# Attention, two feed-forwards and a decaying memory on one core: weights enter the scans as ratios, the next input is made ready early, and ScalarE squares what it rectifies

## The reference

```python
x = x + _layernorm(_L0_attn_ref(_layernorm(x), ...))   # attention
x = x + _layernorm(_L0_ffn_ref(_layernorm(x), ...))    # first feed-forward
x = x + _layernorm(_L1_attn_ref(_layernorm(x), ...))   # the memory
x = x + _layernorm(_L1_ffn_ref(_layernorm(x), ...))    # second feed-forward
```

```python
p_w = jnp.exp(log_p + log_tw)              # a weight per time and slot, 32 slots
phi = k_val[..., None] * theta             # 32 slots x 8 channels x 8 angles
den = jnp.cumsum(p_w[..., 0], axis=1)
num_re = jnp.cumsum(pwb * jnp.cos(phi), axis=1)
num_im = jnp.cumsum(pwb * jnp.sin(phi), axis=1)
inv = lax.rsqrt(jnp.maximum(den, 0.0001)); inv = inv * inv
out = jnp.sum(s_re * qr + s_im * qi, axis=-1)   # s = num * inv; likewise out_im
y = silu(y_re + y_im) @ W_out
```

## Time and profile before

| | us |
|---|---|
| median of 3 runs | 1694.96 |
| lowest, highest | 1694.31, 1700.07 |
| the profiled execution's own time | 1691.56 |
| its span, first to last instruction | 1689.7 |

### The profile page before, as it was taken

The page is one execution under the profiler, slowest core; times in us unless marked ns, Lnnn a source line. Parts: engine busy times, 40 slices in busy tenths (PEclk is TensorE's granted clock), DMA queues, the critical chain, the costliest instruction groups (busy, mean ns, idle before and its releaser), DMA issues.

```text
span 1689.7 us, 22269 instructions
## 1 busy us (share of the span) xinstructions
PE 1298.3 (77%) x7692; PEld 792.9 (47%) x7692; DVE 1330.3 (79%) x2794; ACT 960.4 (57%) x1637; POOL 564.5 (33%) x335
## 2 busy tenths in 40 slices
PE   4376886678779987988789988897799877865336
PEld 2244364435445554646455654564456455422214
DVE  4953347988788889987998899987989899778850
ACT  2165357744685578565865687457855794343301
POOL 1000301472054602570246314540546035505600
PEclk9589898779979998989899999999899989877668
DMA  5310223103311322131313131222203320012000
GB/s 181 75 38 1 63 45 100 59 24 83 87 60 38 75 65 88 38 87 38 95 57 77 31 100 59 68 52 63 96 25 75 71 82 26 13 61 78 13 0 13
DMA packets 62431, 101.38 MB, mean 60 GB/s; under 512 B 8192, under 2 KB 32144, under 8 KB 62320
## 3 DMA queue, kind: packets, MB, share of 16 engines
q1 hardware_dynamic: 62320, 99.95, 21.4%
HBM read 74.24 MB, written 25.69 MB: 59 GB/s over the span
## 4 chain that ended last, share of the span: by engine, by line
PE 33%; DVE 22%; ACT 12%; issue 12%; POOL 10%; DMA 8%; SPq 2%; POOLq 0%; DVEq 0%; ACTq 0%
PE ps L752 13%; PE ps L762 10%; POOL work L719 5%; DVE work L1304 4%; DVE work L1223 4%; DVE work L1313 3%; ACT work L1001 3%; DMA work<-weights 2%; ACT work L1008 2%; DVE norms L1134 2%; PE ps L833 2%; DMA work<-values 2%; POOL norms L687 2%; PE ps L815 2%; PE ps L890 2%
## 5 line engine op out<-in xcount | busy, mean ns | idle before, releaser
L719 POOL TENSOR_TENSOR work<-work 128x1024 f32<-128x1024 f32 x128 | 336.5, 2654 | 480.9 <-ACT work L1056 400.3
L1001 ACT ACTIVATE work<-work 128x384 f32<-128x384 f32 (+3 forms) x512 | 264.7, 558 | 168.7 <-DVE work L1223 167.8
L1304 DVE TENSOR_TENSOR_SCAN work<-ps,work 128x512 f32<-128x512 f32 x256 | 302.2, 1209 | 17.5 <-POOL work L719 17.0
L1223 DVE CUSTOM_DVE_ANT_0 work<-ps,work 128x384 f32<-128x384 f32 (+3 forms) x512 | 226.8, 485 | 109.1 <-PE ps L807 106.5
L815 PE MATMUL ps<-ident,work 128*128 128x128 f32 x1280 | 217.3, 298 | 53.8 <-DVE work L1223 44.5
L687 POOL TENSOR_TENSOR norms<-norms,power 128x4 f32<-128x4 f32 x64 | 71.3, 1114 | 498.8 <-DVE norms L1140 498.7
L815 PEld LDWEIGHTS ps<-ident,work 128*128 128x128 f32 x1280 | 160.1, 152 | 130.1 <-DVE work L1223 77.2
L1313 DVE TENSOR_TENSOR work<-work 128x1024 f32<-128x1024 f32 x128 | 215.2, 1681 | 5.1
L1008 ACT COPY work<-ps 128x512 f32<-128x512 f32 x320 | 181.2, 571 | 46.3 <-PE ps L815 46.2
L807 PE MATMUL ps<-work 96*128 96x384 bf16 (+3 forms) x512 | 132.5, 327 | 47.8 <-ACT work L1008 39.3
L752 PE MATMUL ps<-xTd,wf 128*128 128x512 f32 x256 | 126.0, 629 | 11.5 <-ACT xTd L966 7.9
(11 more groups left out here) (161 smaller groups left out, 1937.5 us busy)
## 6 DMA issues: line engine op xcount, KB each, us to landing
work<-values SPq DMA_DIRECT2D x64, 256.0 KB
work<-weights SPq DMA_DIRECT2D x64, 256.0 KB
scratch<-work SPq DMA_DIRECT2D x32, 384.0 KB, 5.1
work<-scratch SPq DMA_DIRECT2D x64, 192.0 KB, 3.7
work<-scratch SPq DMA_DIRECT2D x64, 128.0 KB, 4.0
x_in<-x SPq DMA_DIRECT2D x8, 512.0 KB, 3.4
work<-scratch SPq DMA_DIRECT2D x64, 64.0 KB, 4.0
weights<-work SPq DMA_DIRECT2D x8, 512.0 KB, 4.6
```

The source lines that it names most:

```text
L719: g_.tensor_tensor(wave, wave, pwr[:, slot, None, :].to_broadcast([P, MH, T]), ALU.mult).then_inc(*weighed[half].one)
L1001: i = s_.activation(part_of, part_of, ACT.Exp, scale=-1.0, bias=nmax[:, row:row + 1])
L1223: i = v_.tensor_tensor_reduce(sc[:, n % 4, at:at + nk], out_of(name)[:, at:at + nk], base_of(qt), -SCORE_SCALE, BIG, ALU.add, ALU.min, nma ...
L1304: v_.tensor_tensor_scan(ring[:, at, m, :], still.to_broadcast([P, T]), ring[:, at, m, :], 0.0, ALU.add, ALU.add).then_inc(*scanned.one)
```

## The change

It has these parts:

- **Ratios in the scans.** The weighted sum n(t) = n(t-1) + w(t) c(t) is replaced by s(t) = s(t-1) * w(t-1)/w(t) + c(t), so s = n / w. The scan reads the ratio from `pwr` (SBUF) and multiplies; `weigh` goes. The factor at the gate is now w / sum of w. The weights are bounded from below by 1e-20 so that they can divide.
- **Where ratios come from.** `total`: VectorE bounds the weights, scans and bounds their sum. SP stores both and loads them back spread over 128 partitions x 128 times, the weights twice, the second time one element earlier (`spread`). `ratio`: two reciprocals and two products of 128x128. SP stores the ratios in four pieces and the rates (`rates`), then loads the four `pwr` slots. A slot is free after the scans of its sine half.
- **Next input early.** `x_in` has two buffers; x[b+1] is loaded during attention b (`fetch`), its statistics and centring come near the end of the score tiles (`stats+`, `centre+`), its scaling and transposes around the output product (`norm+`, `xT+`). The output's statistics have a chain of their own in `norms`.
- **First feed-forward.** ScalarE squares right after rectifying, GpSimd no longer. The head of b + 2 (`fstats`, `fnorm`, `fxT`) stands before the last product of b, and `fnorm` waits for the transposes of b - 2 only.
- **q and k pieces** go to DRAM separately, q before k is computed.
- **Start.** Only `wo` is centred ahead (`means` 0, `N_WO` = 3 steps); the first output product waits for that alone. The rest of the preparation is interleaved with the first attention. In b = 0 every second transposed score tile is copied out by VectorE (20 copies).
- PSUM banks 5 and 6 are dealt out in program order over both dense halves, and `MERGE` is written anew for all engines.

```diff
@@ items
-    items = ["stats", "norm", "xT", "ckv", ("q", 0), ("q", 1), "qr", ("k", 0), ("k", 1), "kr", "pieces", ...
+    items = ["ckv", ("q", 0), ("q", 1), ("pieces", 0), "qr", ("k", 0), ("k", 1), ("pieces", 1), "kr", ...
+        if n == ALL - 4:
+            items += ["stats+", "centre+"] * after
+    items += ["attnT"] + ["norm+"] * after + ["out"] + ["xT+"] * after + ["ystats", "sum"]
...
-def on_act(m):
-    return True
+def on_act(b, m):
+    return b > 0 or m % 2 == 0
@@ MERGE, one line of each engine's
-        "a5 p10 a3 p12 a90 d a15 d a4 d a4 d a18 d a5 d a4 d a4 d a4 m2 a4 m2 a3 m a4 m2 a4 m2 a2 m2 a2 m a2 "
...
@@ SP
-                if item == "weights":
-                    need(sp, pw_ready, b, 1)
-                    sp.dma_start(weights[b], zs[:, None].to_broadcast([K, H, T])).then_inc(*p_saved.one)
+                if item == "total":
+                    need(sp, w_ready, b, 1)
...
+                    sp.dma_start(plain[1 + b * K * T:1 + (b + 1) * K * T].rearrange("(k t) -> k t", k=K), zs).then_inc(*w_saved.one)
+                    need(sp, tot_ready, b, 1)
+                    sp.dma_start(totals[b], total).then_inc(*tot_saved.one)
+                if item == "spread":
+                    need(sp, kv_saved[0], b, 1)
+                    need(sp, w_saved, b, 2)
+                    for before in (1, 0):
+                        at = 1 - before + b * K * T
+                        sp.dma_start(spread[:, 1 - before, :], plain[at:at + K * T].rearrange("(p t) -> p t", p=P)
+                                     ).then_inc(*spread_loaded.one)
+                    need(sp, tot_saved, b, 1)
+                    sp.dma_start(spread[:, 2, :], totals[b].rearrange("k (i t) -> (k i) t", i=TT)).then_inc(*spread_loaded.one)
+                if item == "rates":
+                    need(sp, ratio_ready, b, 1)
+                    for i in range(TT):
+                        sp.dma_start(ratios[b, :, :, i * P:(i + 1) * P],
+                                     spread[i:P:TT, 0, None, :].to_broadcast([K, H, P])).then_inc(*ratio_saved.one)
+                    need(sp, rate_ready, b, 1)
+                    sp.dma_start(rates[b].rearrange("k (i t) -> (k i) t", i=TT), spread[:, 2, :]).then_inc(*rate_saved.one)
@@ POOL
-                if item == "fc":
-                    is_drained(pool, b, f"fc{n}")
-                    g_.tensor_tensor(hid[:, n, :], hid[:, n, :], hid[:, n, :], ALU.mult).then_inc(*hid_sq.one)
-                if item == "weigh":
...
-                    g_.tensor_tensor(wave, wave, pwr[:, slot, None, :].to_broadcast([P, MH, T]), ALU.mult
-                                     ).then_inc(*weighed[half].one)
@@ PE, first output product
-                        pe.wait_ge(prep_step, N_PREP)
+                        pe.wait_ge(prep_step, N_WO)
@@ ACT
                 if item == "fnorm":
-                    need(act, g_sum, b - 2, 1)
+                    if b:
+                        is_filled(act, *((b - 2, "gxT1") if b > 1 else (0, "zxT1")))
...
+                    is_drained(act, b, f"fc{n}")
+                    s_.activation(hid[:, n, :], hid[:, n, :], ACT.Square, bias=zero[:, 0:1]).then_inc(*hid_sq.one)
@@ DVE
-                if item == "inv" and n == 0:
-                    need(dve, pw_ready, b, 1)
+                if item == "total":
+                    need(dve, exp_ready, b, 1)
+                    v_.tensor_scalar(zs, zs, LEAST, None, ALU.max).then_inc(*w_ready.one)
...
-                    step(inv_step, v_.tensor_scalar(total, total, 1e-4, None, ALU.max))
-                    v_.reciprocal(total, total).then_inc(*inv_ready.one)
+                    v_.tensor_scalar(total, total, 1e-4, None, ALU.max).then_inc(*tot_ready.one)
+                if item == "ratio":
+                    need(dve, spread_loaded, b, 3)
+                    before, now, den, per = (spread[:, i, :] for i in range(4))
+                    v_.reciprocal(den, den)
+                    step(ratio_step, v_.reciprocal(per, now))
+                    v_.tensor_tensor(before, before, per, ALU.mult).then_inc(*ratio_ready.one)
+                    v_.tensor_tensor(den, den, now, ALU.mult).then_inc(*rate_ready.one)
...
-                    need(dve, weighed[half], b, r + 1)
-                    v_.tensor_tensor_scan(ring[:, at, m, :], still.to_broadcast([P, T]), ring[:, at, m, :], 0.0,
-                                          ALU.add, ALU.add).then_inc(*scanned.one)
+                    need(dve, (cos_waved, sin_waved)[half], b, r + 1)
+                    need(dve, pw_loaded[slot], b, use)
+                    v_.tensor_tensor_scan(ring[:, at, m, :], pwr[:, slot, :], ring[:, at, m, :], 0.0,
+                                          ALU.mult, ALU.add).then_inc(*scanned.one)
```

More of the change, by code:

```diff
@@ L23 @@
 REP = K // KQ
+ZS = 64
 ML = 4
@@ L243, with __init__ @@
+    for chain in "ad":
+        for b, item, n in chains()[chain]:
+            for name in names(item, n):
+                if name != "zs":
+                    last[chain] = (last[chain] + 1) % 3 if chain == "a" else 11 - last[chain]
+                use(b, name, last[chain])
+    for b in range(B):
+        use(b, "mem0", 7), use(b, "mem1", 7)
+    return place, uses
 class Signal:
-    def __init__(self, sem, per_batch, step=1):
+    def __init__(self, sem, per_batch, step=1, total=None):
```

444 lines of the change are left out of this document (231 added, 213 removed), and 71 rows, old and new, of the table MERGE.

## The result

| | before | changed |
|---|---|---|
| median of 4 runs, us | 1695.95 | 1649.05 |
| lowest to highest | 1694.31 to 1700.07 | 1645.58 to 1650.25 |
| span of the profiled execution | 1689.7 | 1646.3 |

The ratio is 0.972, with a 95% interval from 0.969 to 0.974. The change saves 46 us and the forecast was 113. At 1649 the time lies just outside the range of 1525 to 1645.

A forecast was written before the change was run, and what follows sets the result against it. The prediction took VectorE as the bound, with TensorE close. Terms A -16, B -14, C -81, D -12 and E +10 gave -113 us against 1691.56, so 1579 us; own range 1555 to 1605, whole range 1525 to 1645.

The forecast's parts named there:

- Term D: Waits for GpSimd go (-17, -7), the ratio's longer round trip through DRAM adds 12: -12 us, bounds -24 to +64.
- the fourth rival: VectorE waits at `ratio` for the spread load, 20 us in each sequence: slower, 1737 us, chance 0.04.
- Term C: VectorE's busy time falls by 93 us, counted at its 87% share: -81 us, bounds -93 to -27.
- Term B: Next input made ready early closes a 16.6 us gap in attention, counted once: -14 us, bounds -16 to 0.
- Squares, costed at nothing: First feed-forward's squares move from GpSimd to ScalarE, hidden by ScalarE's idle third: 0 us, bounds -4 to +44.
- Term A: At the start, the first score tile moves to about 66 us, 8 us of moved work showing: -16, bounds -24 to -4.
- Term E: Scans, now with two operands in SBUF, collide with GpSimd's remaining work: +10 us, bounds 0 to +29.
- The first, TensorE as the bound: TensorE can't get above 88% in the middle, so 17 us are saved there and not 51: 1613 us, chance 0.22.
- The third, the long `mix` coming back: VectorE's long `mix` have other causes or the scans bring them back; 7 of C is left: 1652 us, chance 0.07.

The follow-up runs named there:

- kv_behind: The changed kernel with SyncE issuing a sequence's first four value loads behind the stores and spread loads of the weights' sums: 1602.79 us, ratio to before 0.945.
- before_small_weigh: The kernel before with GpSimd's weighing cut to one of 512 times, all waits and the number of instructions kept: 1681.87 us.
- sq_pool: The changed kernel with the squares of the first feed-forward on GpSimd again in place of ScalarE: 1669.00 us.
- weigh_back: kv_behind with the 16 weighings of a sequence put back on GpSimd ahead of the scans, which keep the ratio as well: 1785.89 us.
- input_late: The changed kernel with the next input's statistics, centring and scaling put back behind the sum of the sequence before: 1705.41 us, ratio to before 1.006.
- kv_input_late: kv_behind with the next input late in the same way as in input_late: 1660.13 us.
- copies_act: The changed kernel with all transposed score tiles copied out by ScalarE, those of the first sequence too: 1648.77 us.

## Why the prediction was wrong

**Term D, the round trip, is the step that put the time outside the range.** The prediction took 4.6 us for the store, from a store of 512 KB in another place of the queue, and +12 us in all, with VectorE's wait at the ratio under 2 us a sequence. The store took 9.6 to 12.2 us behind the value loads, the wait was 6.2 us a sequence, and kv_behind, where the same store is fast, is 46 us quicker. What stands ahead of a transfer in its queue was taken as nothing. The mechanism, a wait at `ratio` for a slow round trip, is that of the fourth rival, at a third of the price it was given. With the fast store the time is 1602.8, 24 us above the forecast and inside the range. In the same term VectorE's 17.0 us of waits at the scan were to go. The scan waits 37.8 us now, for the cosine.

That the forecast comes so near with the fast store is in part luck: the early input and the squares gave 76 us where 14 were counted, and that makes up for part of what terms A and C didn't give.

**Term C had the work right and its worth wrong.** `mix`, `frac` and `turn` lost 78 us against 85 forecast, and the reciprocals and products with the new bound some 4 of at most 8 (the reciprocal, interpolated at 949 ns, took 954 and 895). The step "0.87 x 93", VectorE's share of the time as the worth of its work, failed: before_small_weigh gives 14 us for 69 us of VectorE's work (0.2), sq_pool pays 20 for 28.6 (0.7) and weigh_back 183 for 182 (1.0). Taking work out of the old order opened idle time, and adding work to the new one cost most or all of it. VectorE's share of the time, 0.87, foretold none of these.

**Term B was mis-sized.** "I count it once" gave 14 us. input_late and kv_input_late give 56 and 57, 8 us for each of seven changes of sequence. Other chains did not cover the gap: before the change it was 23 to 29 us at every one of the seven, and now it is 10 to 15.

**Squares, costed at nothing (at most 4 us either way)**: 20 us gained in the new order, 11 lost in the old. ScalarE's share came out as forecast (70% in the middle, 722 ns for a square), but what the squares did to others was left out: on GpSimd they lengthen VectorE's work by 28.6 us, which is the likely source of the 20, and in the old order ScalarE's idle third was no cover.

**Term A.** The first score tile came at 65.5 us, as forecast, but 4 us were left at the first output product and not 16. copies_act shows that the copies do not explain it. The step that failed is that the moved work would come in the gaps between score tiles, with 8 us showing. The trace has it in two blocks without a score tile: the tables from 73.45 to 81.0 us and the centring from 82.39 to 94.8, 20 us together. ScalarE then waits 12.26 us for its next score tile and TensorE 10.98 for VectorE's next copy:

```profile
73.45 0.28 DVE L1445 TENSOR_TENSOR work<-work 128x128 f32<-128x128 f32 x1
82.39 2.28 DVE L1480 TENSOR_REDUCE work<-wpr 128x8 f32<-128x2048 f32 x1
96.26 0.91 ACT L1032 ACTIVATE work<-work 128x384 f32<-128x384 f32 x2 [12.26 <-DVE work L1262]
95.69 1.93 PE L863 MATMUL ps<-work 128*32 128x128 f32 x32 [10.98 <-DVE work L1208]
```

The granted clock from the first score tile to the output product is also lower, 0.82 in place of 0.96. No run spread the blocks out, so what that would give back is not shown.

**Term E.** +5.5 us of work on the scans and about 6 us of time, against +10 in bounds of 0 to 29. The collision is there (single scans up to 3.3 us), but small, since GpSimd is busy 10% of the time; beside the weighing in weigh_back it is 97 us.

**The rivals.** The first, TensorE as the bound, gave 1613 and 17 us saved in the middle. The changed kernel saved 6 there, for another reason (TensorE was at 86%, and kv_behind gave more), so that its time lies nearer is chance. For kv_behind the rival is not ruled out: TensorE is at the 88% that it named as the limit, and 1603 lies nearer to 1613 than to 1579. Against it, the middle takes 845 us and not 868, and VectorE's wait at the score tile, which it wanted grown, is 29.1 us there in place of 40.3. The third, the long `mix` coming back, gave 1652, and that this is nearly the time measured is chance too: `mix` is at 1.23 us, as forecast.

The parts do not add up to the 46 us: the early input 56, the squares 20, the weighing 174 beside the new scan, less 46 for the store. Each was priced in the new order. In the old one the two that could be tried alone give 14 us and -11, together 5. The gain is of the parts and the new order together; how much the order alone gives, with the separate q and k pieces and the banks dealt out anew, was not tried.

## What to carry to other kernels

In an order written by hand an engine's busy share doesn't say what its work is worth: here taking 69 us of work out of the old order gave 14. Try the part alone in the old order, and cut the span at the same instructions before and after, to see in which stretches the time goes down. Before a new round trip through DRAM is priced, list what its queue holds ahead of it; a small store behind up to 1 MB of loads took 10 to 12 us, and moving the loads behind it was worth as much as the whole change. A gap at the change from one sequence to the next should be counted each time unless a row shows what fills it. And work that is moved into gaps has to be cut into pieces that fit them: 20 us of preparation in two blocks took most of what the earlier first score tile had gained.

## What the runs showed of the hardware

A scan with both operands in SBUF is lengthened by GpSimd's work as a product is (mean 1.61 us in weigh_back, 1.23 in kv_behind, single ones up to 3.4), where one with an operand in PSUM stays at 1.21 beside the same weighing. Pressed this way GpSimd is slower too, but little: in one row five weighings took 16.3 us, 3.26 each, and over all 128 the mean is 2.76 us against 2.65 in the kernel before.
